# Key products of two blocks by terms, and a new order of all engines in a loop over batch entries

## The chip, the cores and the metric

The kernel runs on one core of one Trainium2 chip. The metric is the device time of one execution in microseconds, here the median of several executions. TensorE is called PE (its weight loads PEld), VectorE DVE, ScalarE ACT, GpSimd POOL, SyncE SP.

## The reference

One layer of cross attention and a quantized feed-forward network, for 32 batch entries of 100 tokens of width 256, with a context of 361 rows per entry and 16 heads of 64:

```python
x = x + xattn(layernorm(x), ctx, ctx, WQ, WK, WV, WO, mask)   # softmax(Q K^T / 8 + mask * -1e9) V, then WO
x = x + ffn(layernorm(x), W1, b1, W2, b2)                     # per-tensor 8 bit codes, exact gelu
```

The ranges from which the feed-forward network takes its codes are taken over all of its input and all of its hidden values, so it starts only when the attention of all 32 entries is done.

## The kernel before, in words

Every f32 operand of the attention is split into two f16 halves (`_h`, `_l`), and a product is three products, high by high, high by low and low by high, that accumulate in one PSUM bank (`split3`, L376 to L378). Three stages follow each other: the query projections of all entries (to about 87 us), the attention, one entry per turn (to 972 us), and the feed-forward network.

A **turn** is written as steps, and all of its PE steps are:

- K0 to K7: keys of two heads each (bank of 362 columns, six products: `k` = 0, 1 over the two halves of the width, three terms each). ACT writes the high half of the keys (L789), DVE the low one (L1096), and only then is the bank free.
- V0 to V5: values, 128 or (V2, V5) 105 context rows by 512 columns, six products each; ACT L793, DVE L1102 read them.
- QP0 to QP7: the scores of two heads, two products of 64 rows side by side, three times (L1401). A score step of DVE, MAX (L1042), reads one head's; ACT takes the exponential (L779), the high half of the probabilities (HA, L785; for heads 2, 5, 8, 11 and 14 DVE does it, HV, L1049), POOL the low half (LO, L626), and SP transposes two heads by DMA (DT).
- PV0 to PV15: probabilities by values, nine products of 65 columns a head (L1423); NORM, AH, AL and AD bring them to WO0, WO1, the output projection, twelve products of 256 columns each.
- CT: one product for the scale of the next context (L1289), called the probe here. It is there once a turn.

The context of a turn arrives by DMA, POOL scales it, ACT rounds it to `ctx_h` (C, L829, two halves, `s_ch`), and POOL subtracts to `ctx_l` (C, L615, `s_c`). K, V and WO share **two PSUM banks in turn** (`bank_of`): a step takes the bank of the step two before it in that row, and `bank_read` waits for DVE's read of that one. In the loop of before the row is K0 to K3, V0, V1, V2, K4, K5, V3, K6, WO0, K7, WO1, V4, V5.

What sets the order is a table of times for each engine (`PE_STEPS`, `ACT_STEPS` and so on, L88 to L133). `turn` sorts the steps of a table by time and cuts the circle at `CUT`; steps of negative time belong to the next entry. The tables give the part before the loop ("first"), the loop's body ("whole", 31 times), and the `LAST_` lists the part behind it. Each engine runs its own row in order and waits on semaphores alone, so the order decides who waits. The PE row of the loop before (steps of the next entry with a +, the probe of the entry after it with ++):

```
PV6 PV7 K0+ K1+ PV8 PV9 K2+ K3+ QP0+ QP1+ V0+ V1+ PV10 CT++ PV11 QP2+ QP3+ V2+ K4+ PV12 to PV15
K5+ V3+ QP4+ QP5+ K6+ WO0 PV0+ K7+ WO1 V4+ V5+ PV1+ PV2+ QP6+ QP7+ PV3+ PV4+ PV5+
```

In the last part no transposing DMA is used for heads 10 to 15: PE transposes their probabilities (PT), and ACT or DVE copies them (PC).

Of the kernel before, what the change touches and what calls it, by code (L numbers as in the profile page):

```python
# [18 lines left out]
F16 = mybir.dt.float16  # L19
# [63 lines left out]
def at(**times):  # L83
# [23 lines left out]
DVE_STEPS = at(
    K=(-5.893, -5.648, -4.835, -3.797, -0.261, 0.688, 2.418, 4.814),
    V=(-2.725, -2.274, -0.679, 1.492, 6.435, 6.987),
    WO=(19.53, 20.987),  # L110
    MAX=(-3.586, -3.558, -3.405, -3.008, -1.096, -0.776, 0.566, 0.613, 2.019, 3.178, 4.599, 6.349, 7.567, 8.998,
        10.111, 10.476),
    HV=(-1.157, 1.45, 4.284, 7.744, 10.491),
    NORM=(7.591, 9.855, 13.495, 16.606),
    CMAX=(-20.735,),
    CRED=(-17.097,),
    SCALE=(-14.336,),
    LN=(21.337, 21.523, 25.402, 25.985))
# [59 lines left out]
def build(nc, x, ctxT, mask, wq, wk, wv, wo, w1T, b1, w2T, b2, out):  # L178
# [528 lines left out]
    def _(act):  # L707
# [175 lines left out]
    def _(dve):  # L883
# [148 lines left out]
        def dve_turn(b, part):  # L1032
            banks = bank_of(part)
            for kind, n, later in order(DVE_STEPS, part, LAST_DVE):
# [223 lines left out]
    def _(pe):  # L1258
# [94 lines left out]
        def bank_read(kind, n, a):  # L1353

            if kind == "K":
                wait(pe, s_k, NP_ * a + n + 1)
            elif kind == "V":
                wait(pe, s_v, 2 * ST * a + n + 1)
            else:
                wait(pe, s_x1, 2 * a + n + 1)  # L1360

        def pe_turn(b, part):
# [3 lines left out]
            for kind, n, later in order(PE_STEPS, part, LAST_PE):  # L1366
                a, ps = b + later, banks.get((kind, n))
                if ps is not None:
                    g = jobs.index((kind, n, later))
# [5 lines left out]
                if kind == "K":  # L1375
                    ms = slice(n * P, (n + 1) * P)
                    for k in range(KD):
                        if n == 0:
                            wait(pe, s_c, KD * a + k + 1)
                        ins = split3(pe, ps[:, 0:SE], (wk_h[:, k, ms], wk_l[:, k, ms]),  # L1380
                                     (ctx_h[:, k, :], ctx_l[:, k, :]), k == 0, k == KD - 1)
# [26 lines left out]
                elif kind == "PV":  # L1408
                    j, half = n // GH, n // HT
                    if part != "last" or n < 10:  # L1410
                        pe.wait_ge(s_dt[n % RT // 2], 16 * (H // RT * a + n // RT + 1))
                    else:
                        copied = [m for kind_, m in (LAST_ACT if n in (11, 13) else LAST_DVE) if kind_ == "PC"]
                        pe.wait_ge(s_pca if n in (11, 13) else s_pcd, copied.index(n) + 1)
                    if n % GH == 0:
# [10 lines left out]
                elif kind == "PT":  # L1426
                    if n < 12:
                        wait(pe, s_v, 2 * ST * (a + 1))
                    if n == 14:
# [10 lines left out]
                elif kind == "AT":  # L1440
                    if n == 3:
                        pe.wait_ge(s_dal, 1)
                    else:
                        wait(pe, s_al, NG * a + n + 1)
                    pe.wait_ge(*((s_pcd, 2), (s_pca, 2), (s_pcd, 3), (s_pcd, 4))[n])
                    for c in range(4):
# [3 lines left out]
                elif kind == "WO":  # L1450
# [121 lines left out]
```

## Time and profile before

| | us |
|---|---|
| median of 3 executions (1068.87 to 1070.16) | 1069.17 |
| the profiled execution: its own time | 1070.84 |
| its span, first to last instruction | 1068.8 |
| PE busy in the span | 1028.5 (96%) |
| DVE, ACT, POOL busy | 928.9, 868.4, 784.7 |
| granted clock of PE in the loop | 1.00 of full |
| share of PE in the chain that ended last | 91% |

A product is shown from its start to a modelled end that reaches into the next one, so an engine that is called busy all the time can still start a product late; the distance from start to start tells it. The profiled execution's time is 1.7 us over the median.

### The profile page before, as it was taken

How to read it: one execution, taken by the hardware profiler on the slowest of the kernel's cores; microseconds unless marked ns; L12 is line 12 of the kernel's file. 1: busy time of each engine (PE TensorE's matmuls, PEld its weight loads, DVE VectorE, ACT ScalarE, POOL GpSimd, SP SyncE). 2: the span in 40 equal slices, each digit the busy share in tenths (PEclk: the TensorE clock that was granted, in tenths of full speed). 3: DMA queues.
4: the chain of work that ended last, by engine and by line, in shares of the span. 5: the costliest groups of instructions: out<-in, count | busy, mean ns of one | idle time of the engine just before them, and what ended most of it. 6: DMA issues, size and time to landing. Idle time of an engine off the chain costs nothing.

```text
span 1068.8 us, 38364 instructions
## 1 busy us (share of the span) xinstructions
PE 1028.5 (96%) x10935; PEld 661.2 (62%) x10935; DVE 928.9 (87%) x2741; ACT 868.4 (81%) x1828; POOL 784.7 (73%) x1116
## 2 busy tenths in 40 slices
PE   7999999999999999999999999999999999997658
PEld 6665666666666666666666666666666666665227
DVE  6887888888889888888888889888888888887897
ACT  4765888888888888888888888888888888875865
POOL 2356877877777887877777877787787877774680
PEclk9999999999999999999999999999999999999989
DMA  8402676766777666667677666776667666663003
GB/s 249 136 1 52 126 138 137 140 137 138 142 142 142 138 138 138 137 138 141 142 142 142 138 137 138 141 141 137 137 139 138 139 137 138 138 133 128 1 0 124
DMA packets 435440, 136.81 MB, mean 128 GB/s; under 512 B 407666, under 2 KB 434390, under 8 KB 435414
## 3 DMA queue, kind: packets, MB, share of 16 engines
q1 hardware_dynamic: 435414, 136.47, 61.2%
q8 instruction: 15, 0.25, 0.1%
q14 instruction: 11, 0.09, 0.0%
HBM read 28.60 MB, written 6.55 MB: 33 GB/s over the span
## 4 chain that ended last, share of the span: by engine, by line
PE 91%; DVE 3%; ACT 2%; issue 2%; POOL 1%; DMA 0%; SPq 0%; DVEq 0%; ACTq 0%; POOLq 0%
PE front L376 21%; PE front L378 18%; PE front L377 18%; PE back L1423 13%; PE front L1401 7%; PE tp L1401 5%; PE front L1538 1%; ACT q_all L869 1%; PE back L378 1%; PE back L377 1%; PE back L376 1%; PE tp L1342 1%; PE front L1268 1%; PE tp L1538 0%; PE back L1538 0%
## 5 line engine op out<-in xcount | busy, mean ns | idle before, releaser
L626 POOL TENSOR_TENSOR hl<-prob,hl 100x361 f16<-100x361 f32 x511 | 428.6, 853 | 74.0 <-ACT hl L785 73.2
L779 ACT ACTIVATE prob<-prob,nmax 100x361 f32<-100x361 f32 x512 | 295.3, 589 | 5.1 <-DVE nmax L1042 3.7
L1423 PEld LDWEIGHTS back<-v,pT 128*128 128x128 f16 (+1 forms) x4608 | 167.8, 98 | 32.3 <-issue 9.6
L785 ACT ACTIVATE hl<-prob 100x361 f16<-100x361 f32 x352 | 175.4, 498 | 3.4
L1423 PE MATMUL back<-v,pT 128*128 128x65 f16 (+1 forms) x4608 | 176.9, 193 | 0.8 <-DMA pT<-hl 0.8
L789 ACT ACTIVATE k_h<-front 128x362 f16<-128x362 f32 x256 | 120.1, 469 | 63.8 <-PE front L378 59.9
L376 PE MATMUL front<-ctx_h,wk_h 128*128 128x362 f16 x512 | 164.0, 320 | 1.6 <-DVE v L1102 1.0
L378 PE MATMUL front<-ctx_h,wk_l 128*128 128x362 f16 x512 | 161.7, 316 | 0.0
L377 PE MATMUL front<-ctx_l,wk_h 128*128 128x362 f16 x512 | 161.4, 315 | 0.0
L1102 DVE SCALAR_TENSOR_TENSOR v<-front,v 128x512 f16<-128x512 f32 (+1 forms) x192 | 132.6, 691 | 32.2 <-ACT v L793 31.5
L793 ACT ACTIVATE v<-front 128x512 f16<-128x512 f32 (+1 forms) x192 | 114.4, 596 | 55.4 <-PE front L378 49.8
L1042 DVE CUSTOM_DVE_ANT_0 prob<-tp,mask_g,ngain 100x361 f32<-100x361 f32 x256 | 147.9, 588 | 10.7 <-POOL hl L626 7.5
L1042 DVE CUSTOM_DVE_ANT_0 prob<-front,mask_g,ngain 100x361 f32<-100x361 f32 x256 | 148.5, 590 | 5.7 <-POOL hl L626 0.3
L376 PE MATMUL front<-wv_h,ctx_h 128*128 128x512 f16 (+1 forms) x384 | 147.6, 384 | 1.7 <-DVE k_l L1096 1.2
L377 PE MATMUL front<-wv_l,ctx_h 128*128 128x512 f16 (+1 forms) x384 | 145.5, 379 | 0.0
L378 PE MATMUL front<-wv_h,ctx_l 128*128 128x512 f16 (+1 forms) x384 | 145.5, 379 | 0.0
L1096 DVE SCALAR_TENSOR_TENSOR k_l<-front,k_h 128x362 f16<-128x362 f32 x256 | 135.8, 530 | 6.5 <-ACT k_h L789 3.0
L630 POOL TENSOR_TENSOR ahl<-att,ahl 100x256 f16<-100x256 f32 x127 | 85.1, 670 | 36.6 <-ACT ahl L799 36.6
L615 POOL TENSOR_TENSOR ctx_l<-ctx_raw,ctx_h 128x361 f16<-128x361 f32 x64 | 53.1, 853 | 44.3 <-ACT ctx_h L829 44.3
L1049 DVE TENSOR_SCALAR_CACHE_REDUCE hl<-prob 100x361 f16<-100x361 f32 x160 | 83.8, 524 | 0.7 <-ACT prob L779 0.7
L376 PEld LDWEIGHTS front<-ctx_h,wk_h 128*128 128x128 f16 x512 | 49.7, 97 | 46.8 <-POOL ctx_l L615 9.7
L376 PEld LDWEIGHTS front<-wv_h,ctx_h 128*128 128x128 f16 (+1 forms) x384 | 41.1, 107 | 59.1 <-issue 19.1
(220 smaller groups left out, 2090.8 us busy)
## 6 DMA issues: line engine op xcount, KB each, us to landing
ctx_raw<-ctxT SPq DMA_DIRECT2D x33, 361.0 KB, 3.1
pT<-hl SPq DMA_TRANSPOSE x253, 3.6
xs<-x SPq DMA_DIRECT2D x8, 400.0 KB
q_all<-x SPq DMA_DIRECT2D x32, 100.0 KB
out<-q_all SPq DMA_DIRECT2D x32, 100.0 KB
xb<-out SPq DMA_DIRECT2D x5, 640.0 KB, 8.5
out<-xb SPq DMA_DIRECT2D x25, 128.0 KB, 1.7
q_all<-wq SPq DMA_DIRECT2D x1, 1024.0 KB, 6.2
```

The lines of the kernel that those rows point to most:

```text
L376: eng.matmul(dst, lh, rh, start=first, stop=False)
L377: eng.matmul(dst, lh, rl, start=False, stop=False)
L378: return eng.matmul(dst, ll, rh, start=False, stop=final)
L626: pool.tensor_tensor(hl[0:T, n % RT, 1, 0:S], prob[0:T, n % RP, 0:S], hl[0:T, n % RT, 0, 0:S], ALU.subtract).then_inc(s_lo, 1)
L779: act.activation(prob[0:T, n % RP, 0:S], prob[0:T, n % RP, 0:S], ACT.Exp, bias=nmax[0:T, n:n + 1], scale=-1.0).then_inc(s_exp, 1)
L785: act.activation(hl[0:T, h % RT, 0, 0:S], prob[0:T, h % RP, 0:S], ACT.Copy).then_inc(s_ha, 1)
L789: act.activation(k_h[:, n % 4, :], ps[:, 0:SE], ACT.Copy, scale=KS).then_inc(s_kh, 1)
L1042: dve.tensor_tensor_reduce(prob[0:T, n % RP, 0:S], ring[n % RP][0:T, 0:S], mask_g[0:T, 0:S], ngain[0:T, 0:1], 3.0e38, ALU.add, ALU.min, nm ...
L1096: dve.scalar_tensor_tensor(out=k_l[:, n % 4, :], in0=ps[:, 0:SE], scalar=KS, in1=k_h[:, n % 4, :], op0=ALU.mult, op1=ALU.subtract).then_in ...
L1102: dve.scalar_tensor_tensor(out=v[:, 1], in0=ps[0:rows_of(n), :].rearrange("p (h d) -> p h d", h=HT), scalar=VS, in1=v[:, 0], op0=ALU.mult, ...
L1401: ins = pe.matmul(ring[(2 * n + h) % RP][:, 0:SE], qs[rows[h], n, :], ks[rows[h], n % 4, :], start=t == 0, stop=t == 2)
L1423: ins = pe.matmul(obank[j % 2][:, n % GH * DV:(n % GH + 1) * DV], pT[0:r, n % RT, part_ * ST + st, :], v2[half][0:r, st, v, n % HT, :], st ...
```

## The change

All five tables and the `LAST_` lists are new. The new PE row of the loop:

```
QP6 QP7 PV4 PV5 K0+ K1+ PV6 to PV9 K2+ QP0+ QP1+ K3+ PV10 PV11 V0+ V1+ CT++ PV12 QP2+ QP3+ PV13 K4+
PV14 PV15 V2+ K5+ QP4+ V3+ QP5+ K6+ PV0+ WO0 WO1 K7+ V4+ PV1+ PV2+ V5+ PV3+
```

The row of the two banks is now K0 to K3, V0, V1, K4, V2, K5, V3, K6, WO0, WO1, K7, V4, V5. K0 and K1 are one step by terms: first the four products of each that take `ctx_h`, then the two of each that take `ctx_l`; the waits for `ctx_l` stand in front of the latter, and K1's bank is asked for in front of K1's first product. In the last part PE transposes heads 12 to 15 alone; the DMA for heads 10 and 11 and the load of the last `x` have moved into the loop, and QP6, QP7, PV4 and PV5 of the last entry stand behind it. Core of the diff:

```diff
 PE_STEPS = at(
-    K=(-4.984, -4.872, -3.617, -3.61, 0.002, 1.727, 3.279, 6.846),
+    K=(-4.663, -4.662, -4.044, -3.204, -0.118, 3.617, 5.381, 7.212),
...
-LAST_PE = [("PV", n) for n in range(6, 10)] + [
-    ("PT", 10), ("KW", 0), ("PT", 11), ("KW", 1), ("PT", 12), ("KW", 2), ("PT", 13), ("PT", 14), ("PV", 10), ("PV", 11),
-    ("PT", 15), ("PV", 12), ("PV", 13), ("AT", 0), ("PV", 14), ("PV", 15), ("AT", 1), ("WO", 0),
-    ("AT", 2), ("AT", 3), ("WO", 1)]
+LAST_PE = [("QP", 6), ("QP", 7)] + [("PV", n) for n in range(4, 10)] + [
+    ("KW", 0), ("PT", 12), ("KW", 1), ("PT", 13), ("PV", 10), ("PV", 11), ("KW", 2), ("PT", 14), ("PT", 15),
+    ("PV", 12), ("PV", 13), ("AT", 0), ("PV", 14), ("PV", 15), ("AT", 1), ("WO", 0), ("AT", 2), ("AT", 3), ("WO", 1)]
...
+                def bank_free(g):
...
+                        bank_read(had[0], had[1], b + had[2])
+                if (kind, n) == ("K", 1):
+                    continue
+                if ps is not None:
+                    g = jobs.index((kind, n, later))
+                    bank_free(g)
+                if kind == "K" and n == 0:
+                    assert jobs[g + 1] == ("K", 1, later)
+                    two = [(banks[("K", m)], slice(m * P, (m + 1) * P)) for m in range(2)]
+                    for m, (dst, ms) in enumerate(two):
+                        if m == 1:
+                            bank_free(g + 1)
+                        for k in range(KD):
+                            if m == 0:
+                                wait(pe, s_ch, KD * a + k + 1)
+                            pe.matmul(dst[:, 0:SE], wk_h[:, k, ms], ctx_h[:, k, :], start=k == 0, stop=False)
+                            pe.matmul(dst[:, 0:SE], wk_l[:, k, ms], ctx_h[:, k, :], start=False, stop=False)
+                    for m, (dst, ms) in enumerate(two):
+                        for k in range(KD):
+                            if m == 0:
+                                wait(pe, s_c, KD * a + k + 1)
+                            ins = pe.matmul(dst[:, 0:SE], wk_h[:, k, ms], ctx_l[:, k, :], start=False, stop=k == KD - 1)
+                        ins.then_inc(s_kp, 1)
...
-            if part == "first":
-                for had in jobs[-2:]:
-                    bank_read(had[0], had[1], b + had[2])
+            assert part != "first" or turn(JOBS, "whole")[-2:] == jobs[-2:]
```

Three places of the order. The first is PE at the top of the loop's body, before (names: `v_0_105` is the first half of the values, `s_v`, `s_c` and `s_ch` are the semaphores of V's bank, the low and the high context halves):

```order
L1423 MATMUL back<-v_0_105,pT 128x65 [waits s_dt3]
L1423 MATMUL back<-v_0_105,pT 128x65 x8
L382 ISA
L382 ISA [waits s_v]
L376 MATMUL front<-ctx_h,wk_h 128x362 [waits s_c]
L377 MATMUL front<-ctx_l,wk_h 128x362
L378 MATMUL front<-ctx_h,wk_l 128x362
L382 REGISTER_ALU
L376 MATMUL front<-ctx_h,wk_h 128x362 [waits s_c]
L377 MATMUL front<-ctx_l,wk_h 128x362
L378 MATMUL front<-ctx_h,wk_l 128x362
```

and of the change:

```order
L1388 MATMUL front<-ctx_h,wk_h 128x362 [waits s_ch]
L1389 MATMUL front<-ctx_h,wk_l 128x362
L381 REGISTER_ALU
L1388 MATMUL front<-ctx_h,wk_h 128x362 [waits s_ch]
L1389 MATMUL front<-ctx_h,wk_l 128x362
L381 REGISTER_ALU
L1388 MATMUL front<-ctx_h,wk_h 128x362 [waits s_v]
L1389 MATMUL front<-ctx_h,wk_l 128x362
L1388 MATMUL front<-ctx_h,wk_h 128x362
L1389 MATMUL front<-ctx_h,wk_l 128x362
L1394 MATMUL front<-ctx_l,wk_h 128x362 [waits s_c] x2
L1394 MATMUL front<-ctx_l,wk_h 128x362 x2
```

K0's second half waited for `s_c` behind three products; the low context products now stand behind eight products of the high one. The second place is PE around QP4 and QP5, before:

```order
L382 REGISTER_ALU [waits s_k,s_q]
L1401 MATMUL front<-k_h,q_h 128x362 [waits s_max]
L1401 MATMUL front<-k_h,q_h 128x362
L1401 MATMUL front<-k_l,q_h 128x362 x2
L1401 MATMUL front<-k_h,q_l 128x362 x2
L382 REGISTER_ALU
L382 REGISTER_ALU [waits s_k]
L1401 MATMUL tp<-k_h,q_h 128x362 [waits s_max]
L1401 MATMUL tp<-k_h,q_h 128x362
L1401 MATMUL tp<-k_l,q_h 128x362 x2
L1401 MATMUL tp<-k_h,q_l 128x362 x2
```

and of the change:

```order
L1420 MATMUL front<-k_l,q_h 128x362 x2
L1420 MATMUL front<-k_h,q_l 128x362 x2
L381 REGISTER_ALU
L375 MATMUL front<-wv_h,ctx_h 128x512 [waits s_v]
L376 MATMUL front<-wv_l,ctx_h 128x512
L377 MATMUL front<-wv_h,ctx_l 128x512
L375 MATMUL front<-wv_h,ctx_h 128x512
L376 MATMUL front<-wv_l,ctx_h 128x512
L377 MATMUL front<-wv_h,ctx_l 128x512
L381 REGISTER_ALU
L381 REGISTER_ALU [waits s_k]
L1420 MATMUL tp<-k_h,q_h 128x362 [waits s_max]
```

V3 has moved between the two query steps, and QP4 follows K5. The third is DVE at the top of the body, before:

```order
L1096 SCALAR_TENSOR_TENSOR k_l<-front,k_h 128x362
L382 ISA
L382 REGISTER_ALU
L1042 ISA prob,nmax<-tp,mask_g,ngain 100x361
L1042 ISA nmax 100x1
L382 REGISTER_ALU
L1096 SCALAR_TENSOR_TENSOR k_l<-front,k_h 128x362
L382 REGISTER_ALU x2
L1042 ISA prob,nmax<-tp,mask_g,ngain 100x361
L1042 ISA nmax 100x1
L382 REGISTER_ALU
L1049 TENSOR_SCALAR hl,hsum<-prob 100x361
```

and of the change:

```order
L1095 SCALAR_TENSOR_TENSOR k_l<-front,k_h 128x362
L381 ISA
L381 REGISTER_ALU
L1041 ISA prob,nmax<-tp,mask_g,ngain 100x361
L1041 ISA nmax 100x1
L381 REGISTER_ALU x2
L1048 TENSOR_SCALAR hl,hsum<-prob 100x361
L381 REGISTER_ALU
L1095 SCALAR_TENSOR_TENSOR k_l<-front,k_h 128x362
L381 REGISTER_ALU
L1086 RECIPROCAL rinv<-back 100x4
```

Before, two score steps and one HV step stood among K0, K1 and K2; now one score step (head 15) and the HV step of head 14 stand between K0 and K1, and the NORM of heads 4 to 7 follows K1.

## Rows read from the trace of the kernel before

**Rows 1.** Windows, loop and end: busy of PE, PEld, DVE, ACT, POOL; clock; DMA

```profile
121.20:940.60 819.40, 818.62 (x9035) 525.53 (x9032) 731.83 (x2281) 704.53 (x1561) 656.02 (x931) 1.00 0.69 139
940.60:972.00 31.40, 28.16 (x400) 21.16 (x396) 24.77 (x77) 21.54 (x46) 19.70 (x28) 1.00 0.44 88
```

**Rows 2.** The waits: who waited for whom; us in total, times, longest

```profile
PEld front L376 <- DVE k_l L1096: 17.9, 64, 1.7
PEld front L376 <- POOL ctx_l L615: 9.7, 30, 0.5
```

**Rows 3.** Timeline, PE: the probe of one turn and the next; start, us, what

```profile
312.69 0.30 PE L1289 MATMUL front<-ident,cmax 128*128 128x128 f32 x1
...
340.00 0.30 PE L1289 MATMUL front<-ident,cmax 128*128 128x128 f32 x1
```

**Rows 4.** Timeline, PE, same turn: where a product starts late

```profile
314.23 0.42 PE L376 MATMUL front<-wv_h,ctx_h 128*105 128x512 f16 x1
314.48 0.38 PE L377 MATMUL front<-wv_l,ctx_h 128*105 128x512 f16 x1
...
323.17 0.44 PE L1423 MATMUL back<-v,pT 128*128 128x65 f16 x9
323.45 0.32 PE L376 MATMUL front<-ctx_h,wk_h 128*128 128x362 f16 x1
...
325.57 0.27 PE L378 MATMUL front<-wo_h,attT 128*100 128x256 f16 x1
325.86 0.39 PE L376 MATMUL front<-wv_h,ctx_h 128*128 128x512 f16 x1
...
331.83 0.32 PE L378 MATMUL front<-ctx_h,wk_l 128*128 128x362 f16 x1
332.09 0.33 PE L376 MATMUL front<-ctx_h,wk_h 128*128 128x362 f16 x1
...
333.48 0.71 PE L1423 MATMUL back<-v,pT 128*128 128x65 f16 x18
334.11 0.33 PE L376 MATMUL front<-ctx_h,wk_h 128*128 128x362 f16 x1
```

**Rows 5.** Timeline, PE, same turn: into and out of a query pair

```profile
319.59 0.38 PE L378 MATMUL front<-wv_h,ctx_l 128*128 128x512 f16 x1
319.90 0.33 PE L1401 MATMUL front<-k_h,q_h 64*128 64x362 f16 x2
...
320.68 0.32 PE L1401 MATMUL tp<-k_h,q_l 64*128 64x362 f16 x2
320.93 0.33 PE L376 MATMUL front<-ctx_h,wk_h 128*128 128x362 f16 x1
```

**Rows 6.** Timeline, ACT, same turn: V2, the two context halves, K0

```profile
315.76 0.60 ACT L793 ACTIVATE v<-front 105x512 f16<-105x512 f32 x1 [0.39 <-PE front L378]
...
329.69 0.90 ACT L829 ACTIVATE ctx_h<-ctx_raw 128x361 f16<-128x361 f32 x2
...
332.93 0.47 ACT L789 ACTIVATE k_h<-front 128x362 f16<-128x362 f32 x1 [0.23 <-PE front L378]
```

**Rows 7.** Timeline, DVE, same turn: V2 and K0

```profile
316.39 0.69 DVE L1102 SCALAR_TENSOR_TENSOR v<-front,v 105x512 f16<-105x512 f32 x1
...
333.52 0.53 DVE L1096 SCALAR_TENSOR_TENSOR k_l<-front,k_h 128x362 f16<-128x362 f32 x1
```

**Rows 8.** Groups of the loop, DVE: a score step; busy, mean ns | idle

```profile
L1042 DVE CUSTOM_DVE_ANT_0 prob<-front,mask_g,ngain 100x361 f32<-100x361 f32 x240 | 139.2, 590 | 5.1
```

**Rows 9.** Timeline, POOL, same turn: both low halves of the context

```profile
330.38 1.66 POOL L615 TENSOR_TENSOR ctx_l<-ctx_raw,ctx_h 128x361 f16<-128x361 f32 x2 [1.44 <-ACT ctx_h L829]
```

**Rows 10.** Timeline, PE, before the loop

```profile
89.95 0.33 PE L376 MATMUL front<-ctx_h,wk_h 128*128 128x362 f16 x1 [0.47 <-DVE k_l L1096]
...
100.17 0.33 PE L376 MATMUL front<-ctx_h,wk_h 128*128 128x362 f16 x1 [0.99 <-DVE v L1102]
```

**Rows 11.** Timeline, PE, behind the loop

```profile
964.16 0.44 PE L1434 MATMUL front<-identb,hl 100*128 100x100 f16 x6 [0.97 <-POOL hl L626]
```

More of the change, by code:

```diff
@@ L107 @@
-DVE_STEPS = at(
[L108 to L118, printed above, removed]
@@ new lines @@
+    V=(-1.994, -1.687, 2.259, 3.715, 7.498, 9.763),
+    QP=(-3.626, -3.625, -1.277, -1.276, 3.714, 3.716, 10.034, 10.035),
+    PV=(5.422, 7.872, 8.554, 9.892, 10.987, 11.197, 11.407, 11.438, 11.738, 11.892, 13.032, 13.931, 14.722,
+        15.545, 17.127, 17.603),
+    WO=(21.804, 22.073),
+    CT=(-17.279,))
+ACT_STEPS = at(
+    K=(-4.216, -3.657, -2.821, -1.327, 3.993, 5.693, 6.045, 7.638),
+    V=(0.873, 2.351, 4.587, 5.952, 8.468, 9.799),
+    EXP=(-2.297, -0.88, -0.647, 3.478, 4.175, 4.256, 5.767, 6.126, 6.141, 6.889, 8.346, 8.439, 10.716, 11.643,
+        12.183, 12.803),
+    HA=(-0.825, 3.192, 3.838, 4.57, 6.032, 6.532, 7.599, 9.116, 11.135, 12.025, 13.29),
+    AH=(11.13, 16.48, 19.229, 21.667),
+    YN=(25.76,),
+    MG=(-3.333,),
+    C=(-5.862, -5.853),
+    Q=(-5.553, -1.309))
@@ new lines @@
+DVE_STEPS = at(
+    K=(-5.615, -5.351, -3.23, -0.901, 1.751, 3.113, 4.495, 8.306),
+    V=(0.275, 0.496, 2.997, 3.958, 8.768, 9.242),
+    WO=(21.857, 22.257),
+    MAX=(-3.882, -3.059, -1.231, -0.693, 0.796, 0.988, 2.059, 3.647, 3.801, 4.992, 5.456, 6.523, 9.212, 9.329,
+        9.674, 10.424),
+    HV=(0.546, 3.738, 6.169, 8.513, 10.482),
+    NORM=(9.188, 11.389, 15.791, 17.789),
+    CMAX=(-16.754,),
+    CRED=(-15.205,),
+    SCALE=(-11.519,),
+    LN=(22.935, 23.603, 25.262, 25.558))
+SP_STEPS = at(
+    DT=(-1.359, 1.676, 2.409, 3.851, 6.037, 7.821, 12.765, 12.997),
+    AD=(16.275, 16.719),
+    CTX=(-21.874,),
+    OUT=(23.248,),
+    X=(7.673,))
@@ L134 @@
+POOL_STEPS = at(
+    LO=(-1.494, 0.913, 1.642, 2.414, 2.753, 4.811, 6.596, 8.018, 8.18, 8.932, 9.666, 9.739, 11.403, 11.514,
+        11.95, 12.74),
+    AL=(12.242, 15.918, 18.272, 18.716),
+    C=(-5.637, -5.592),
+    Q=(-5.115, -0.324),
+    RSTD=(25.387,),
+    CS=(-8.551,),
+    M=(17.325,))
 JOBS = {step: t for step, t in PE_STEPS.items() if step[0] in ("K", "V", "WO")}
@@ L315, in build @@
     tpb = [tp[n][:, :].bitcast(F16) for n in range(2)]
-    last_bank = {n: (proj[n % 2] if n < 12 else ring[n % RP]).bitcast(F16) for n in range(10, H)}
+    last_bank = {n: ring[n % RP].bitcast(F16) for n in range(12, H)}
     att_bank = [ring[n].bitcast(F16) for n in range(NG)]
@@ L1374, in pe_turn @@
                         bank_read(had[0], had[1], b + had[2])
-                if kind == "K":
+                if (kind, n) == ("K", 1):
[20 more added lines that the diff above has]
+                        ins.then_inc(s_kp, 1)
+                elif kind == "K":
                     ms = slice(n * P, (n + 1) * P)
                     for k in range(KD):
-                        if n == 0:
-                            wait(pe, s_c, KD * a + k + 1)
                         ins = split3(pe, ps[:, 0:SE], (wk_h[:, k, ms], wk_l[:, k, ms]),
@@ L1409, in pe_turn @@
                     j, half = n // GH, n // HT
-                    if part != "last" or n < 10:
+                    if part != "last" or n < 12:
                         pe.wait_ge(s_dt[n % RT // 2], 16 * (H // RT * a + n // RT + 1))
                     else:
-                        copied = [m for kind_, m in (LAST_ACT if n in (11, 13) else LAST_DVE) if kind_ == "PC"]
-                        pe.wait_ge(s_pca if n in (11, 13) else s_pcd, copied.index(n) + 1)
+                        copied = [m for kind_, m in (LAST_ACT if n == 13 else LAST_DVE) if kind_ == "PC"]
+                        pe.wait_ge(s_pca if n == 13 else s_pcd, copied.index(n) + 1)
                     if n % GH == 0:
```

47 lines of the change are left out of this document (7 added, 40 removed), and 4 rows, old and new, of the table LAST_DVE.

## The prediction

> **What bounds the kernel now.** I read the busy time by stretch first. In the loop, 819.40 us of the span, PE is busy for 818.62 [rows 1]; DVE has 731.83, ACT 704.53, POOL 656.02. So nothing that one of those three does is worth anything unless it lets PE start a product sooner, and PE's own work can't shrink, for the change removes no product inside the loop. The clock is 1.00 throughout. The chain of waits agrees: 91% of it is PE (table above).
>
> But "busy" hides late starts, because a product's shown end reaches into the next one. So I went to the starts. One turn, probe to probe, takes 340.00 - 312.69 = 27.31 us [rows 3]. The list of waits names what PE's weight loads stand for: DVE's low half of the keys (64 times) and POOL's `ctx_l` (30 times) [rows 2]. That is once or twice a turn. In the timeline each is a start that comes later than its spacing allows. Normal spacings follow from the same rows: a key product 0.154 (nine of them from 332.09 to 333.48), a head of PV 0.28 (323.17 to 323.45), an output product 0.11, a value product 0.154 x 512/362 = 0.22 [rows 4].
>
> **What the change takes away, per turn.**
> - K0's second half waits for `ctx_l`: 332.09 - 331.83 - 0.15 = 0.11 [rows 4]. POOL's two halves begin at 330.38 and last 1.66, to 332.04 [rows 9], which is just ahead of that start.
> - K2 waits for K0's bank: from 333.48 two heads of PV need 0.55, K2 comes 0.63 later [rows 4]: 0.08. DVE's read of K0 ends at 333.52 + 0.53 = 334.05 [rows 7], K2 starts at 334.11.
> - V4 waits for K7's bank: 325.86 - 325.57 - 0.11 = 0.18 [rows 4]. In the new row of banks V4 follows WO1's bank, with K7 (six products, 0.92) in between, and DVE reads an output in one step, without ACT before it.
> - V2 right behind a query pair has its second product 0.25 after its first [rows 4], 0.03 over the spacing. Now PV15 is in front of it.
>
> Together 0.40.
>
> **What it gives back, per turn.** A query step packs two products of 64 rows. Going in costs 319.90 - 319.59 - 0.22 = 0.09, coming out 320.93 - 320.68 - 0.15 = 0.10 [rows 5]. Before, the eight query steps ran in four groups; now QP4 and QP5 have V3 between them, so there are five: +0.19. The Trainium skill has the rule for this, "TensorEngine Tiling (Array Packing)", Key Properties: changing the tiling mode drains TensorE. The trace agrees that a switch costs, and the rule speaks against this edit. Read with "TensorE: Matmul & The Clock Gate", Single matmul latency, which puts the fixed part of a warm product at about 166 ns, two whole drains would be an estimated 0.33 a turn, and the net of a turn would be about nothing; the rows above have measured the switch itself, and the sum goes by them.
>
> V3 now takes the bank of V2, with K5 and QP4 between: 0.92 + 0.09 + 0.47 + 0.10 = 1.58 us from V2's end. To free the bank ACT must start (0.20 after V2's end, which is where K4 starts, 315.56 by V2's 314.48 and five spacings), work 0.60 [rows 6], then DVE 0.69 [rows 7] and a signal of 0.04 or so between engines: 1.57. This has no margin, and whether the 0.10 of coming out of the pair runs beside the wait isn't shown anywhere: between 0 and 0.10, and I take 0.06, over the middle, as DVE has a score step in front of V2 whose 0.59 [rows 8] leaves little. K2 stays tight as well: it now comes 0.31 (K1's last two products) + 4 x 0.28 = 1.42 after K0's end, while the read of K0 took from 332.09 + 3 x 0.154 = 332.55 to 334.05, 1.50, before. There DVE was kept by the steps ahead; ACT's start at 332.93 plus 0.47 [rows 6], 0.04, and DVE's 0.53 would have allowed 333.97, or 1.42. So 0 to 0.08; I take 0.02, near the end that the durations give.
>
> Sum: -0.40 + 0.19 + 0.06 + 0.02 = **-0.13 a turn**, with ends at -0.21 (neither wait) and -0.03 (both in full). Over the 30 turns from the loop's first probe to its last: -3.9 (-0.9 to -6.3).
>
> **Where covers have moved.** By terms is not a gain of its own; it pays for the new place of K0. Before, K0 came 331.83 - 0.31 = 331.52, i.e. 3.07 us after V5's end (325.86 + 12 x 0.216 = 328.45). Now only PV3, QP6, QP7, PV4, PV5 lie between: 0.28 + 0.09 + 0.93 + 0.10 + 0.55 = 1.95. ACT takes V5 0.20 after its end and the first context half 0.49 behind that; from there to POOL's last result is 332.04 - 329.69 = 2.35 [rows 6, 9]. So `ctx_l` is there 3.04 after V5's end. With the old order of products K0 would want it at 1.95 + 0.46 = 2.41 and stand 0.63 us; by terms the second half is wanted at the tenth product, 1.95 + 9 x 0.154 = 3.34. It is covered with 0.3 to spare. The bank of K1 is V5's: ACT to 0.80, then DVE's 0.69 behind the score step of head 12, which can't begin before QP6 is through (0.28 + 0.09 + 0.47 + 0.20 = 1.04) and takes about 0.5 of DVE. That is 2.3 after V5's end, later than K0's start at 1.95 and ahead of K1's first product at 2.57. Asked at K0 it would have cost 0.35; asked where it is now, nothing.
>
> **Before and behind the loop.** In front of the loop nothing stands between K1 and K2. K2 already waits there (0.47 idle) for K0 [rows 10], and K0 is now complete with its tenth product instead of its sixth: +0.61. The fifth query group adds 0.19. The wait of 0.99 for V2's bank [rows 10] mostly goes, as V2 now stands behind K4 and K5's bank is K4's: -0.7, and new short ones at V0 and V1 (up to 0.3) come. I take +0.4 (0 to +0.9). Behind the loop, 31.40 us in which PE has 3.2 idle [rows 1], the last scores are what counts: PE stands 0.97 for the low half of head 13 [rows 11]. DVE used to have NORM0, HV3, NORM1 ahead of the last score steps and now has one value step in their place, about 1 us less; but the copies, PV10 to PV15, and the two output halves follow as before, with their own waits. I take -0.4 (+0.3 to -1.1). Nothing in the feed-forward part changes.
>
> **Total.** -3.9 + 0.4 - 0.4 = -3.9. Against the profiled execution that is 1070.84 - 3.9 = 1066.9; it lies 1.7 over the median, so for the median 1069.17 - 3.9 = **1065.3**. The sums of the bounds are -7.4 and +0.3; they don't all fall together, and the forecast's own range is 1062.9 to 1067.5. What a measurement of this kernel can tell from no change is about 0.2%, 2.1 us, so up to 1067.0 is faster and from 1071.3 slower.
>
> **Rivals.**
> 1. *The tight waits don't bind.* DVE and ACT are free when V2 and K0 end. Then -0.21 a turn, -6.3, and +0.4 - 0.4 around it: 1062.9. For it: both waits came out near zero from durations alone. Against it: DVE and ACT are busy 89% and 86% of the loop, and a step that is ready seldom finds its engine idle.
> 2. *The margins are eaten.* Margins of 0.3, 0.3 and 0.2 stand where there were small waits. If DVE or POOL runs 0.2 later at one or two of them, the turn gains nothing: 1068 to 1070. That the new question for K1's bank, or the terms, do nothing because the data come early anyway leads to the same place. For it: before the change, every such wait was under 0.2 too, and a shift of the same size decides.
> 3. *Slower, at QP1.* DVE now has K0, the score of head 15, HV of head 14, then K1. QP1 needs K1's low half. From K1's last product QP1 is 4 x 0.28 + 0.92 + 0.09 + 0.47 = 2.60 away; DVE's row for it is 0.40 (K0's start) + 0.45 + 0.51 + 0.44 + 0.57 = 2.37. HV needs the exponential of head 14, which ACT does behind K0's high half and one copy: about 1.3 against the 1.36 at which DVE wants it. HV may come 0.3 late before PE stands. From there every 0.1 us costs 3 us of the kernel; at 0.53 late PE stands 0.23 a turn: -3.9 + 6.9 = +3.0, so 1072.2. It decides from about 0.43 late on, where the gain of 0.13 is used up. Against it: ACT has three short steps before that exponential, with their inputs long there.
>
> **Chances.** Forecast 0.52 (of which a tenth lies above 1067.0), the first rival 0.14, the second 0.24, the third 0.10. So faster 0.47 + 0.14 + 0.02 of the second's near end = 0.63, same 0.27, slower 0.10. The range takes in the forecast, the first rival down to a turn of -0.24, and most of the second, leaving out the third and the tails: 1062.0 to 1069.0.
>
> **What would show it.** Probe to probe about 27.18 in place of 27.31. No late start in K0's second half, at V4, or in V2's second product; five entries and five exits of query steps of 0.09 to 0.10; V3 up to 0.1 late behind QP4; K2 within 0.1 of its spacing. In front of the loop K2 idles about 1 us. I am wrong if the turn is under 27.08 or over 27.3, if QP1 or K3 starts late, or if the waits name POOL's `ctx_l` again.

## The result and the profile after

The changed kernel takes 1059.62 us (median of 5, 1058.99 to 1061.76) against 1068.87 for the kernel before (5 more executions, 1066.54 to 1070.16): 0.9923 of it, 95% interval 0.9907 to 0.9939. That is -9.2 us; -3.9 was forecast, and 1059.62 lies 2.4 under the range. The sign was right, the size was not.

The windows of the changed kernel, loop and the stretch behind it (same columns as [rows 1]):

```profile
118.80:931.20 812.40, 812.40 (x9032) 522.34 (x9030) 727.17 (x2280) 705.32 (x1561) 658.59 (x931) 1.00 0.70 140
931.20:962.70 31.50, 28.37 (x372) 21.45 (x371) 23.64 (x74) 19.95 (x43) 19.47 (x29) 0.95 0.46 91
```

The loop has lost 7.0 of its 819.4 us, and PE is busy in all of it. The list of what PE waits for no longer has POOL's `ctx_l`, and DVE's `k_l`, 64 times before [rows 2], is there 6 times, before and behind the loop:

```profile
PEld tp L1420 <- DVE nmax L1041: 13.1, 31, 0.4
PEld front L375 <- DVE v L1101: 9.8, 32, 0.5
...
PEld front L375 <- DVE k_l L1095: 4.2, 6, 1.5
```

The two that stand there 31 and 32 times are weight loads of QP5 and V3 that wait while the product ahead still runs: they cost a start nothing, as the timeline shows. One turn, from probe to probe, with the places of the prediction (columns as in [rows 3, 4]):

```profile
308.43 0.27 PE L1288 MATMUL front<-ident,cmax 128*128 128x128 f32 x1
...
314.35 0.32 PE L1420 MATMUL front<-k_h,q_l 64*128 64x362 f16 x2
314.60 0.39 PE L375 MATMUL front<-wv_h,ctx_h 128*128 128x512 f16 x1
...
315.69 0.38 PE L377 MATMUL front<-wv_h,ctx_l 128*128 128x512 f16 x1
316.00 0.33 PE L1420 MATMUL tp<-k_h,q_h 64*128 64x362 f16 x2
...
321.18 0.32 PE L377 MATMUL front<-ctx_h,wk_l 128*128 128x362 f16 x1
321.33 0.38 PE L375 MATMUL front<-wv_h,ctx_h 128*128 128x512 f16 x1
...
326.44 0.32 PE L1388 MATMUL front<-ctx_h,wk_h 128*128 128x362 f16 x1
...
327.06 0.32 PE L1388 MATMUL front<-ctx_h,wk_h 128*128 128x362 f16 x1
...
327.68 0.78 PE L1394 MATMUL front<-ctx_l,wk_h 128*128 128x362 f16 x4
328.29 1.27 PE L1442 MATMUL back<-v,pT 128*128 128x65 f16 x36
329.40 0.32 PE L375 MATMUL front<-ctx_h,wk_h 128*128 128x362 f16 x1
...
335.51 0.27 PE L1288 MATMUL front<-ident,cmax 128*128 128x128 f32 x1
```

A turn is 335.51 - 308.43 = 27.08, from 27.31 [rows 3]. The twelve products of K0 and K1 take 1.85 us (326.44 to 328.29), without a gap at `ctx_l`; V4 follows K7's last product after 0.15 (321.18 to 321.33), its plain spacing; K2 comes 4 x 0.28 behind 328.29, its spacing too. V3, at 314.60, starts 0.25 after the product before, which is 0.15 and the 0.10 of leaving a query step: no wait is left over there. Over 29 turns that distance is 0.245 to 0.248, and K2 and QP1 too keep theirs within 0.002. The queries still pay 0.09 to go in and 0.10 to come out. Read by steps over twenty turns (rounded, the turn went from 27.30 to 27.08), the 0.22 are: K0's `ctx_l` 0.12, K2's bank 0.07, K3's 0.03 (I hadn't listed it), V4's bank and its first product 0.19, V2's start 0.02, the probe's successor 0.03 and V0 0.01, together 0.47 gone; the fifth query group 0.20 and 0.05 at V3, V5 and WO0, in products that change kind, given back.

How close three of these are is on DVE and POOL, same turn:

```profile
313.85 0.69 DVE L1101 SCALAR_TENSOR_TENSOR v<-front,v 105x512 f16<-105x512 f32 x1 [0.40 <-ACT v L792]
...
326.20 0.69 DVE L1101 SCALAR_TENSOR_TENSOR v<-front,v 105x512 f16<-105x512 f32 x1
328.77 0.54 DVE L1095 SCALAR_TENSOR_TENSOR k_l<-front,k_h 128x362 f16<-128x362 f32 x1 [0.20 <-ACT k_h L788]
```

```profile
325.94 1.67 POOL L614 TENSOR_TENSOR ctx_l<-ctx_raw,ctx_h 128x361 f16<-128x361 f32 x2 [0.16 <-ACT ctx_h L828]
```

V2's bank is free at 314.54 and a signal, V3 starts at 314.60. V5's is free at 326.89, K1 wants it at 327.06. K0's is free at 329.31, K2 starts at 329.40. `ctx_l` is whole at 327.61, its last part is wanted at 327.68 + 0.15 = 327.83. DVE stood idle in front of V2 (0.40) and K0 (0.20), each time for ACT: it was not kept by other work, as I had assumed.

### The profile page after: what moved, and what is told of

It reads as the page before. It is cut to its first block, busy times and chain, and to the rows that moved or that the text cites. A ratio compares the mean times of both kernels' runs of the same rounds, so it can differ in the third digit from the quotient of the medians.

```text
span 1057.4 us, 38397 instructions
## 1 busy us (share of the span) xinstructions
PE 1021.1 (97%) x10923; PEld 656.3 (62%) x10923; DVE 921.4 (87%) x2740; ACT 868.6 (82%) x1827; POOL 788.6 (75%) x1116
## 4 chain that ended last, share of the span: by engine, by line
PE 92%; DVE 3%; ACT 2%; issue 1%; POOL 1%; DVEq 0%; POOLq 0%; ACTq 0%
PE front L375 18%; PE front L376 17%; PE front L377 17%; PE back L1442 14%; PE front L1420 7%; PE tp L1420 6%; PE front L1388 2%; PE front L1389 2%; PE front L1394 2%; PE front L1553 1%; ACT q_all L868 1%; PE back L375 1%; PE back L376 1%; PE back L377 1%; PE tp L1341 1%
## 5 line engine op out<-in xcount | busy, mean ns | idle before, releaser
L778 ACT ACTIVATE prob<-prob,nmax 100x361 f32<-100x361 f32 x512 | 291.0, 587 | 8.0 <-DVE nmax L1041 8.0
L1442 PEld LDWEIGHTS back<-v,pT 128*128 128x128 f16 (+1 forms) x4608 | 174.2, 98 | 50.0 <-issue 9.6
L1442 PE MATMUL back<-v,pT 128*128 128x65 f16 (+1 forms) x4608 | 188.3, 193 | 0.0
L1101 DVE SCALAR_TENSOR_TENSOR v<-front,v 128x512 f16<-128x512 f32 (+1 forms) x192 | 129.6, 689 | 15.4 <-ACT v L792 13.5
L375 PE MATMUL front<-ctx_h,wk_h 128*128 128x362 f16 x384 | 122.7, 319 | 1.2 <-DVE k_l L1095 1.1
L377 PE MATMUL front<-ctx_h,wk_l 128*128 128x362 f16 x384 | 121.3, 316 | 0.0
L376 PE MATMUL front<-ctx_l,wk_h 128*128 128x362 f16 x384 | 121.0, 315 | 0.0
L375 PE MATMUL front<-wo_h,attT 128*100 128x256 f16 x256 | 70.3, 275 | 1.3 <-ACT attT L808 0.7
L376 PE MATMUL front<-wo_l,attT 128*100 128x256 f16 x256 | 69.8, 273 | 0.0
L377 PE MATMUL front<-wo_h,attT 128*100 128x256 f16 x256 | 69.8, 273 | 0.0
```

The source lines that it names most:

```text
L375: eng.matmul(dst, lh, rh, start=first, stop=False)
L376: eng.matmul(dst, lh, rl, start=False, stop=False)
L377: return eng.matmul(dst, ll, rh, start=False, stop=final)
L778: act.activation(prob[0:T, n % RP, 0:S], prob[0:T, n % RP, 0:S], ACT.Exp, bias=nmax[0:T, n:n + 1], scale=-1.0).then_inc(s_exp, 1)
L1101: dve.scalar_tensor_tensor(out=v[:, 1], in0=ps[0:rows_of(n), :].rearrange("p (h d) -> p h d", h=HT), scalar=VS, in1=v[:, 0], op0=ALU.mult, ...
L1442: ins = pe.matmul(obank[j % 2][:, n % GH * DV:(n % GH + 1) * DV], pT[0:r, n % RT, part_ * ST + st, :], v2[half][0:r, st, v, n % HT, :], st ...
```

## Where the rest of the 9.2 us is

All kernels of this study have the same five stages, cut at PE's marks: the probe ahead of the attention, the second probe behind it, the last probe, the last output product. One profiled execution each, us:

| | to the first probe | to the loop | loop | behind it | feed-forward | span |
|---|---|---|---|---|---|---|
| before | 65.93 | 55.31 | 819.41 | 30.98 | 97.12 | 1068.8 |
| before_again | 63.28 | 55.33 | 819.20 | 30.99 | 94.56 | 1063.4 |
| before_third | 64.25 | 55.32 | 819.44 | 30.99 | 94.78 | 1064.8 |
| changed | 63.29 | 55.58 | 812.42 | 31.42 | 94.65 | 1057.4 |
| after_again | 63.56 | 55.59 | 812.46 | 31.68 | 95.48 | 1058.8 |
| after_third | 63.56 | 55.59 | 812.43 | 31.33 | 94.57 | 1057.5 |

> The kernel before once more, for its stages: turn 27.30; the first probe between 63.3 and 66.3 us, from the last probe to the last output product 31.0, the feed-forward part between 94.6 and 97.1. If the early and late stages of the kernel before are always the longer ones (65.9 and 97.1), they belong to the change; if they come down, they were luck.

> The kernel before against itself. Ratio 1.000 within its interval. If the first probe (63.3 to 66.2 us so far, whatever the kernel) and the feed-forward part (94.6 to 97.1) depend on the execution only, this one may fall anywhere between; loop 819.3, from last probe to last output product 31.0.

> The changed kernel, unaltered, once more. Theory A: of the 11.4 us between the two profiled spans only the loop's 7.0 (turn 27.30 to 27.08) belong to the change; the 2.64 us up to the first probe and the 2.5 us of the feed-forward part are luck of one execution (the granted clock fell to 0.57 in 12 to 16 us of the kernel before). Then the turn is 27.08 again, while the first probe lies anywhere between 63 and 66 us and the feed-forward part moves by 1 to 3 us from run to run. Theory B: these stages became shorter through the change: the first probe is at 63.3 within 0.3 again, and the feed-forward part 94.7 within 0.3.

> The changed kernel a third time. If the change owns only the loop and its surroundings (-7.0 + 0.3 + 0.6), the median stands 6 us under the kernel before plus what the luck of a few executions leaves (about 1 us): 1061 to 1062.5. If it owns the first and last stages too: 1059.6 or less, first probe 63.3, feed-forward part 94.7.

The three stages in the middle repeat within 0.4 us and give -6.9 + 0.3 + 0.5 = -6.1 us to the change. The first and the last differ from execution to execution in either kernel: the profiled execution that I forecast from had the longest of both. The start shows it (windows, same columns; the kernel before, then before_again, then the changed kernel):

```profile
8.00:12.00 4.00, 0.67 (x31) 0.57 (x27) 2.22 (x3) 2.07 (x4) 0.20 (x2) 1.00 1.10 251
12.00:16.00 4.00, 4.00 (x70) 3.64 (x71) 2.43 (x8) 1.68 (x4) 0.00 (x0) 0.57 1.04 338
```

```profile
8.00:12.00 4.00, 3.18 (x96) 2.72 (x90) 3.41 (x7) 2.53 (x6) 0.70 (x2) 1.00 1.08 247
12.00:16.00 4.00, 3.63 (x69) 2.19 (x64) 3.95 (x14) 3.20 (x6) 0.79 (x1) 1.00 1.04 342
```

```profile
8.00:12.00 4.00, 3.68 (x114) 3.17 (x110) 3.50 (x7) 2.46 (x5) 0.77 (x2) 1.00 1.08 252
12.00:16.00 4.00, 3.63 (x69) 2.26 (x66) 3.95 (x14) 3.27 (x6) 0.78 (x1) 1.00 1.04 336
```

Where PE was through early with the products that fill the start (158 of its products in 4 to 8 us against 132 and 109), it stood for most of 8 to 12 us, and the granted clock of the next 4 us was 0.57 in place of 1.00. That is the execution, not the kernel: `new_bank_early` and `new_split_q`, two variants of the changed kernel described below, have the same start and their first probe at 66.25 and 66.24. The clock is the smaller part of it. PE went on at 11.94 in the kernel before and at 10.02 in before_again; `new_keep_warm`, which went on at 11.94 too but kept the full clock, has its first probe at 65.20, which leaves 0.7 of the 2.7 us for it. What PE stood for until 11.94, 3.33 us, the trace doesn't name.

In the feed-forward part the granted clock of the kernel before was 0.91, 0.88 and 0.79 in three of the first five stretches of 8 us, and 1.00 in all five in before_again; how much of the 2.6 us that makes wasn't taken apart.

The medians, though, are further apart than 6.1: after_third has 1059.58 against 1067.62 (0.9929, 0.9912 to 0.9946), after_again 1060.65 against 1067.44 (0.9935, 0.9919 to 0.9950), so -8.0 and -6.8 beside the -9.2 above. before_third gave 1068.61, 1.0008 (0.9997 to 1.0020) against itself; before_again, one execution, 1065.42. Some 1 to 3 us of the median stay unplaced. The expectation that the loop alone would give 1061 to 1062.5 fell, and so did the one that first and last stage are always shorter after the change, as before_again has them at 63.28 and 94.56. Whether the kernel before merely meets the long kind of start more often can't be told from so few profiles.

## The experiments

Each ratio below is to the kernel before, which ran in the same rounds; a turn is compared with 27.30 where the kernel before was edited and with 27.08 where the changed one was.

**Products by terms, with the old order and without.** The edits: the new branch for K0 and K1 in the kernel before, and the old `for k in range(KD)` over `split3` in the changed kernel.

```diff
 # old_order_terms
-                if kind == "K":
...
+                if kind == "K" and n == 0:
+                    assert jobs[g + 1] == ("K", 1, later)
...
+                elif kind == "K":
...
-                        if n == 0:
-                            wait(pe, s_c, KD * a + k + 1)
 # new_order_old_products: the same lines, the other way
```

> The kernel before with the products of K0 and K1 by terms and nothing else. K0's wait for ctx_l (0.11) goes, but K0 is complete with its tenth product in place of its sixth, and K2 wants its bank 0.55 after K1: its wait grows from 0.08 to about 0.5. Turn 27.30 - 0.11 + 0.4 = 27.6, about 1078 us: by terms alone is slower. Rival: the terms themselves carry the gain: turn 27.1 to 27.2, 1063 us.

Measured: 1082.76 us, 1.0133 (1.0111 to 1.0155), a turn of 27.72: slower by 0.41 a turn. K0 and K1 run without a gap, and K2 waits for K0's bank 0.61 past its spacing (391.52 + 0.55 = 392.07 to 392.68):

```profile
390.90 0.78 PE L1395 MATMUL front<-ctx_l,wk_h 128*128 128x362 f16 x4
391.52 0.71 PE L1443 MATMUL back<-v,pT 128*128 128x65 f16 x18
392.68 0.33 PE L376 MATMUL front<-ctx_h,wk_h 128*128 128x362 f16 x1 [0.44 <-DVE k_l L1096]
```

> New tables, but K0 and K1 product by product as before (K0's second half wants the rest of the context after three products, K1 asks for its bank at its own start). My reckoning: ctx_l is ready 3.04 us after V5's end and wanted at 2.41, so PE stands about 0.6 us a turn at K0; K2 then finds its bank in time. Turn 27.6 to 27.7, 1076 to 1079 us, slower than before. Rival: the terms do nothing because the data come early anyway: turn 27.08, 1059.6 us.

Measured: 1082.96 us, 1.0145 (1.0130 to 1.0159), a turn of 27.85: by terms is worth 0.77 a turn in the new order, 0.14 more than the 0.63 of my working. Two waits make it up:

```profile
387.38 0.72 PE L1422 MATMUL back<-v,pT 128*128 128x65 f16 x18
388.38 0.33 PE L375 MATMUL front<-ctx_h,wk_h 128*128 128x362 f16 x1 [0.27 <-POOL ctx_l L614]
...
388.69 0.32 PE L377 MATMUL front<-ctx_h,wk_l 128*128 128x362 f16 x1
389.16 0.33 PE L375 MATMUL front<-ctx_h,wk_h 128*128 128x362 f16 x1 [0.15 <-POOL ctx_l L614]
```

I had counted only the second half. The old branch asks for the first half ahead of K0's first product, so K0 starts 0.44 late (388.38 in place of 387.38 + 0.56), and then its fourth product 0.31 late. Neither half of the edit pays alone: in the old order, with two heads of PV in front of K2, the terms cost more than they give, and K0's new place needs the terms.

**K1's bank asked for at K0.**

```diff
                 if kind == "K" and n == 0:
+                    bank_free(g + 1)
...
-                        if m == 1:
-                            bank_free(g + 1)
```

> New tables, products by terms, but K1's bank (V5's) asked for at K0's start. My reckoning: DVE gives it up 2.3 us after V5's end, K0 starts 1.95 after it, so PE would stand about 0.35 us a turn: turn 27.4, about 1070 us. Rival: DVE reads V5 ahead of the score step of head 12, the bank is free by then, and the place of the question is worth nothing: turn 27.08, 1059.6 us.

Measured: 1079.96 us, 1.0106 (1.0089 to 1.0124), a turn of 27.68, +0.60. The mechanism is as I had it, the price is larger:

```profile
388.98 0.72 PE L1441 MATMUL back<-v,pT 128*128 128x65 f16 x18
390.13 0.33 PE L1387 MATMUL front<-ctx_h,wk_h 128*128 128x362 f16 x1 [0.43 <-DVE v L1101]
```

V5's last product starts at 387.37, so by its spacing V5 ends at 387.59. DVE's read of its bank is over at 389.30 + 0.69 = 389.99, 2.40 behind that where I had 2.3, and K0, which stands for it, starts another 0.14 later. In the changed kernel the same read ends at 326.89, 0.45 behind K0's start and 0.17 ahead of K1's: of the 0.61 us between K0's start and K1's first product, about three quarters are needed.

**The term for V4 alone.** WO1 ahead of K7 in the kernel before (the times of ACT and DVE moved with it).

```diff
-    WO=(21.008, 23.04),
+    WO=(21.008, 22.84),
...
-    K=(-4.263, -4.147, -3.523, -1.916, 4.611, 5.891, 7.449, 8.666),
+    K=(-4.263, -4.147, -3.523, -1.916, 4.611, 5.891, 7.449, 9),
...
-    WO=(19.53, 20.987),
+    WO=(19.53, 20.81),
```

> The kernel before with only WO1 put ahead of K7 on PE (and the reads of both on DVE and ACT's part of K7 behind it). The term of my sum taken alone: V4's 0.18 goes, turn 27.12, 1063.7 us. Rival: PE comes to K0 0.18 earlier, or ACT and DVE a little later, and what V4 loses is stood at K0, where ctx_l and its first half are then late: turn 27.3 or over, 1069 us or more.

Measured: 1081.94 us, 1.0126 (1.0102 to 1.0150), a turn of 27.73. V4 does start on its spacing, but K0 is 0.29 late at its start and its fourth product 0.31 late, where the kernel before had 0.11, and WO1 0.15:

```profile
389.80 0.33 PE L376 MATMUL front<-ctx_h,wk_h 128*128 128x362 f16 x1
...
390.12 0.32 PE L378 MATMUL front<-ctx_h,wk_l 128*128 128x362 f16 x1
390.58 0.33 PE L376 MATMUL front<-ctx_h,wk_h 128*128 128x362 f16 x1 [0.15 <-POOL ctx_l L615]
```

The rival stood: a wait taken away here reappears, enlarged, at the next place without slack. Whether PE's earlier arrival or ACT's later K7 does most of it wasn't taken apart.

**What a query group costs.** QP3 behind PV13, six groups:

```diff
-    QP=(-3.626, -3.625, -1.277, -1.276, 3.714, 3.716, 10.034, 10.035),
+    QP=(-3.626, -3.625, -1.277, -0.4, 3.714, 3.716, 10.034, 10.035),
```

> The changed kernel with QP3 put behind PV13: six query groups instead of five, nothing else. If a group costs its entry and its exit as the rows show, turn 27.08 + 0.19 = 27.27 and about 1065.4 us. Rival (two drains of the fixed part of a product, 0.33 a group): turn 27.41, 1069.7 us.

Measured: a turn of 27.29, +0.21, and 1067.63 us, 0.9988 (0.9974 to 1.0002). An entry of 0.10 (368.48 to 368.86 less 0.28), an exit of 0.10 and 0.01 at K4 make it. The first theory stands; two whole drains, an estimated 0.33, don't. The median is 2.2 over the 1065.4 expected, which the turns don't explain; the profiled execution had its first probe at 66.24. The Trainium skill, "TensorEngine Tiling (Array Packing)", Key Properties, has it that changing the tiling mode drains TensorE. The trace agrees that a switch costs, 0.10 each way.

```profile
368.48 0.45 PE L1442 MATMUL back<-v,pT 128*128 128x65 f16 x9
368.86 0.33 PE L1420 MATMUL tp<-k_h,q_h 64*128 64x362 f16 x2
```

**Taking the group back.** QP5 right behind QP4:

```diff
-    QP=(-3.626, -3.625, -1.277, -1.276, 3.714, 3.716, 10.034, 10.035),
+    QP=(-3.626, -3.625, -1.277, -1.276, 3.714, 3.7145, 10.034, 10.035),
```

> The changed kernel with QP5 put right behind QP4, ahead of V3: four groups of query steps instead of five. If an entry and an exit cost what the rows show (0.09 + 0.10) and nothing else binds, turn 27.08 - 0.19 = 26.89 and 1053.9 us. Rival: QP5 comes 1.40 us earlier than DVE's score steps of heads 6 and 7 free its banks, and PE waits at QP5 for as much as it gains or more: turn 27.08 or over, no faster than 1059.6 us.

Measured: 1107.45 us, 1.0375 (1.0360 to 1.0390), a turn of 28.53:

```profile
383.33 0.32 PE L1420 MATMUL front<-k_h,q_l 64*128 64x362 f16 x2
384.73 0.33 PE L1420 MATMUL tp<-k_h,q_h 64*128 64x362 f16 x2 [1.08 <-DVE nmax L1041]
```

QP5 needs the score step of head 7, which stands behind K5 in DVE's row. V3 is between QP4 and QP5 for that reason: the 0.20 of the fifth group pay for 1.24 us at QP5. WO0, that takes V3's bank, stands another 0.39. Three further orders move all engines: V2 comes right behind K4, four heads of PV ahead of K5, so that V3 takes K4's bank or V2's with more room, and head 7's score step is ahead of K5 on DVE. PE's row of the second, and the core of its table:

```
QP6 QP7 PV4 PV5 K0+ K1+ PV6 to PV9 K2+ QP0+ QP1+ K3+ PV10 PV11 V0+ V1+ CT++ QP2+ QP3+ K4+ V2+ PV12 to PV15
K5+ V3+ PV0+ QP4+ QP5+ K6+ WO0 PV1+ WO1 K7+ PV2+ V4+ V5+ PV3+
```

```diff
-    V=(-1.994, -1.687, 2.259, 3.715, 7.498, 9.763),
-    QP=(-3.626, -3.625, -1.277, -1.276, 3.714, 3.716, 10.034, 10.035),
+    QP=(-3.626, -3.625, -1.278, -1.277, 3.716, 5.381, 10.034, 10.035,),
...
+    V=(-1.994, -1.687, -0.455, 3.714, 8.554, 9.763,),
```

> Same products, products of K0 and K1 by terms, but another order of all engines in the loop: V2 ahead of PV12 to PV15, QP4 and QP5 together behind V3, V3 taking the bank of K4, so four query groups in place of five, and the score steps moved to match. Theory (a group costs 0.19 us a turn, nothing new binds): the fifth group's 0.19 goes, and with it the small late starts around V5, WO0 and CT0 (0.02 to 0.03 each): turn 26.85 give or take 0.04, about 1053 us. Rival (as with QP5 put behind QP4 alone): a score step on DVE is late for its bank, and the turn is 27.1 or more.

Measured: 1073.37 us, 1.0036 (1.0019 to 1.0052), a turn of 27.33. PE has the four groups, and lost 0.48 against the forecast in waits of 0.03 to 0.14 at seven places. One of them is V4, that takes WO1's bank: it could have started at 382.93, 0.15 behind K7's last product, and starts at 383.08. On DVE the read of that bank is behind two score steps and ends at 382.54 + 0.48 = 383.02:

```profile
382.03 0.59 DVE L1037 CUSTOM_DVE_ANT_0 prob<-tp,mask_g,ngain 100x361 f32<-100x361 f32 x1
382.54 0.08 DVE L1037 DVE_READ_ACCUMULATOR2_ANT nmax<- 100x1 f32 x1
382.54 0.48 DVE L1118 SCALAR_TENSOR_TENSOR q_all<-front,out_s,q_all 100x256 f32 x1
```

> A second order with four query groups; it differs from the first by more room for DVE: the score step of head 7 ahead of the read of K5 as there, but V0, V1, K7 and the outputs with the scores in another row, PV2 and PV1 further from the steps that want their banks. If the group's 0.19 us can be had and the new order only has to avoid late reads on DVE, turn 26.85 to 26.95, 1053 to 1056 us. Rival: DVE is full, each new order loses as much in waits of 0.03 to 0.14 as the group gives, as in the first: turn 27.1 to 27.3, 1060 to 1070 us.

> A third order with four query groups (PV12 ahead of QP2 as in the changed kernel, V4 behind K7 at once, PV2 ahead of V5). Same two theories as for the second: turn 26.85 to 26.95, or 27.1 to 27.3.

Measured: the second 1053.15 us, 0.9846 (0.9825 to 0.9866), a turn of 26.83; the third 1055.77 us, 0.9873 (0.9852 to 0.9893), 26.93. Both **beat the changed kernel**, the second by 0.25 a turn. So the fifth group wasn't the price of this loop: there are orders in which score steps, banks and products fit with four. Which of the moves was needed wasn't taken apart.

**The clock behind the loop.** The stretch from the last probe to the last output product grew from 30.98 to 31.3 to 31.7. Its windows, 19 to 22, 22 to 25 and 25 to 28 us after the last probe, in the changed kernel:

```profile
950.29:953.29 3.00, 1.22 (x28) 1.05 (x25) 2.71 (x12) 2.64 (x6) 1.50 (x3) 0.98 0.60 112
953.29:956.29 3.00, 2.97 (x40) 2.71 (x39) 0.82 (x2) 1.20 (x3) 2.78 (x4) 0.50 0.02 5
956.29:959.29 3.00, 2.31 (x56) 2.19 (x55) 1.97 (x6) 1.65 (x4) 0.67 (x1) 0.95 0.01 3
```

PE stands 1.78 us for POOL's low half of head 12, and behind that the granted clock is 0.50 of full, the lower of its two levels, for 3 us.

```profile
952.72 0.44 PE L1451 MATMUL front<-identb,hl 100*128 100x100 f16 x6 [1.78 <-POOL hl L625]
```

In the kernel before the largest single idle there is 0.97 [rows 11], and the clock stays 1.00. The edit fills the gap with products whose result isn't used:

```diff
-                    for _ in range(6):
+                    for _ in range((44, 6, 6)[n]):
                         pe.matmul(obank[0][:, 512 - P:512], w1q[:, 0, 0:P], w1q[:, 0, 0:P], start=True, stop=True)
```

> The changed kernel with 44 in place of 6 filling products where PE stands 2.0 us for the last tables behind the loop (19.43 to 21.43 us after the last probe). If the granted clock of 0.64 to 0.82 in the 6 us behind it comes from that idle stretch, the clock stays near 1.00 there and from the last probe to the last output product it is about 30.6 us in place of 31.4 to 31.7, 1058.8 us in all. If the clock has nothing to do with it, the stretch stays 31.4 to 31.7, or grows if the filling products delay the transposes.

```profile
952.19:955.19 3.00, 3.00 (x64) 3.00 (x61) 2.61 (x11) 2.64 (x6) 1.50 (x3) 1.00 0.70 109
955.19:958.19 3.00, 2.95 (x73) 2.68 (x71) 2.39 (x5) 1.20 (x3) 2.75 (x4) 1.00 0.02 5
```

The stretch is 30.23, 1.1 to 1.4 shorter. The median is 1060.08 us, 0.9914 (0.9897 to 0.9931), which can't be told from the changed kernel's. And the idle stretch doesn't always cost: new_split_q has the same one, and its clock holds (30.34 in all):

```profile
959.53:962.53 3.00, 1.22 (x31) 1.05 (x28) 2.81 (x11) 2.44 (x6) 1.30 (x3) 1.00 0.66 124
962.53:965.53 3.00, 2.78 (x71) 2.61 (x69) 1.66 (x4) 1.40 (x3) 2.94 (x4) 1.00 0.02 5
```

Of eight executions with an idle stretch of 1.78 us there (the changed kernel three times, new_order_old_products, new_bank_early, four_groups_c, new_split_q, new_join_q) six show the fall, to 0.50 to 0.67 over 22 to 25 us, and the last two don't. That the filling keeps the clock up therefore rests on two executions, this one and four_groups_b_warm below; the price of the fall, 1.0 to 1.3 us, also on new_split_q, which stood as long and kept its clock.

> The second order with four groups, and 44 filling products behind the loop. If the clock's drop there costs the 1.2 us that the profile of the first try showed, 1053.15 - 1 = 1052.2 us and 30.0 us from last probe to last output product; if not, 1053.2 and no difference to be told.

Measured: 1051.96 us, 0.9858 (0.9842 to 0.9875), and 29.66 us behind the last probe against 31.11. The profile has the gain; the medians, 1.2 apart with executions up to 4.5 apart, can't show it.

## Why the prediction was wrong, point by point

- **What goes, per turn.** 0.40 forecast, 0.47 measured. All four waits were there and went at their size; the missing 0.07 are K3's late start, V4's and V0's first products and the one behind the probe, 0.01 to 0.03 each.
- **The fifth group.** +0.19 forecast, +0.20 measured; a sixth cost 0.21. Right. The 0.05 that V3, V5 and WO0 start slower because another kind of product is ahead of them weren't in the sum.
- **V3 +0.06, K2 +0.02: the step that failed.** Both were 0 in every turn of the loop. I took values over the middle and near the end on the ground that DVE is seldom free. The durations alone had given 1.57 against 1.58 and 1.42 against 1.42, and those were right: DVE waited for ACT at both places. The first rival (tight waits don't bind, -0.21 a turn, 0.14 of the chance) is what happened: -0.22. That it meets to 0.01 is luck, as 0.07 more went and 0.06 more came back than it says. Over 30 turns the two waits are 2.4 of the 3.0 us by which the loop gained more than forecast.
- **Before the loop.** +0.4 forecast, +0.3. K2 idles 1.08 there and V2's wait (0.99 [rows 10]) went, both as said: K5, which now wants K4's bank, starts 0.23 late at 97.44, and V3 0.19 late at 99.23. The 1.06 below is another one, V5 for K7's bank, and was 1.16 before.

```profile
87.92 0.33 PE L375 MATMUL front<-ctx_h,wk_h 128*128 128x362 f16 x1 [1.08 <-DVE k_l L1095]
...
106.51 0.42 PE L375 MATMUL front<-wv_h,ctx_h 128*105 128x512 f16 x1 [1.06 <-DVE k_l L1095]
```

- **Behind it.** -0.4 forecast, +0.5 measured. Without the fall of the clock it is 30.2 to 30.3 us, i.e. -0.7: the order did what I said, and the 1.78 us that PE now stands in one piece were followed by a fall of the clock, and that cost 1.0 to 1.4. I had read [rows 11] as a wait to be paid once.
- **The total.** -3.9 forecast, -6.1 measured in the stages that the change touches. The other 3 us to the 9.2 are no work of the order that the profiles show. I set the sum on the median of three executions, and took a difference of 1.7 between that and the profiled one for an offset; the first and the last stage of this one kernel move by 2.7 and 2.6 us between executions, and a range for a median of five should have been some 1.5 us wider on both sides.
- **The covers.** By terms was said to hide 0.63 and hid 0.77 (the first half's wait was missing); asking early was said to cost 0.35 and cost 0.60 (the read ended 0.1 later, and 0.14 from there to K0's start weren't counted). `ctx_l` had 0.22 to spare in the changed kernel where 0.3 was said. The signs of both, and that the margins behind them hold, were right.
- **The third rival** (QP1 late) didn't happen: QP1 starts 0.149 to 0.150 behind QP0's last product in every turn.

## What to carry to other kernels

Where two durations from the trace meet to 0.01 us, forecast that they meet, and look at the row of the engine in question for what it stood for: an average load of 89% says nothing of that place. A late start in this loop couldn't be priced alone: each of three partial edits, two of them sound by their own term, made it 1.3 to 1.5% slower, while the whole change gained 0.7%. And mark the stages of a kernel that an edit doesn't touch and compare them over several executions before the difference of two profiles is explained.

## What the runs showed of the hardware

An idle stretch of PE of 1.78 us behind the loop was followed by 3 us at a granted clock of 0.50 to 0.67 in six executions and by full clock in two, with nearly the same work around it. A group of query steps between other products costs 0.20 to 0.21 us to enter and leave, whether it holds one step or two.
